# Attention edge pass of a four-layer graph network: LayerNorm sums, variance and power at other places of the step, the edge-row product on VectorE, the segment marks on ScalarE, head scalars on 96 rows

## What is computed

```
s_n, v_n = equivariant_layernorm(s, v)                 # per node: mean and variance of 64 scalars, rms of the vectors
msg = (s_n @ Ws_src)[src] + (s_n @ Ws_dst)[dst]        # the same for the vectors
w1  = rbf @ W_rbf                                      # per edge
m1  = tensor_product(msg, y0, y1, w1)                  # products with the edge's spherical harmonics y
a   = sum(leaky(m1_s @ W_alpha) * alpha_dot)           # 4 heads
ex  = exp(a - segment_max(a, dst)[dst]); den = segment_sum(ex, dst)
val = m1 @ W_val; val_v *= sigmoid(val_s @ Wg); val_s = sigmoid(val_s)
h   = tensor_product(val, y0, y1, w2) @ W_vlin         # head scalars (64) and head vectors (96)
agg = segment_sum(ex / den[dst] * h, dst)              # then a projection, and node + projection(agg)
```

## Time and profile before

| | |
|---|---|
| median of 3 runs | 4730.02 us (4730.01 to 4737.36) |
| the profiled execution | 4743.81 us, span 4742.0 us |
| busy over the span | PE 3709.4 (78%), DVE 3285.3 (69%), ACT 2442.6 (52%), POOL 3346.5 (71%) |
| mean granted TensorE clock | 0.904 |

### The profile page before, as it was taken

The page is one execution under the profiler, slowest core; times in us unless marked ns, Lnnn a source line. Parts: engine busy times, 40 slices in busy tenths (PEclk is TensorE's granted clock), DMA queues, the critical chain, the costliest instruction groups (busy, mean ns, idle before and its releaser), DMA issues. The chain is left out here.

```text
span 4742.0 us, 73825 instructions
## 1 busy us (share of the span) xinstructions
PE 3709.4 (78%) x14102; PEld 1795.8 (38%) x14102; DVE 3285.3 (69%) x8309; ACT 2442.6 (52%) x7488; POOL 3346.5 (71%) x3644
## 2 busy tenths in 40 slices
PE   1999997775999999999910288888798789887665
PEld 0333334553333444444300133333566333333444
DVE  1566666774887898888868545554799455445999
ACT  0233324776555555555457534333699333333777
POOL 1566666997686787788546566666588567666888
PEclk9999998998999999999855589888899898988999
DMA  9222225886454554444379622222798222224886
GB/s 403 67 67 70 67 68 167 275 273 179 115 127 108 127 128 127 127 127 127 88 249 364 229 68 65 67 67 64 240 324 298 70 66 69 66 66 133 251 252 212
DMA packets 585572, 718.24 MB, mean 151 GB/s; under 512 B 79012, under 2 KB 409194, under 8 KB 585224
## 3 DMA queue, kind: packets, MB, share of 16 engines
q1 hardware_dynamic: 492812, 536.17, 37.6%
q0 software_dynamic: 86400, 142.71, 11.0%
q10 hardware_dynamic: 6268, 38.40, 2.0%
HBM read 488.77 MB, written 245.93 MB: 155 GB/s over the span
## 5 line engine op out<-in xcount | busy, mean ns | idle before, releaser
L548 POOL DMA_INDIRECT aggregates<-agg_out,scatter_index x600 | 613.9, 1023 | 402.9 <-issue 247.6
L1296 ACT ACTIVATE y_chunk<-residual,ln_minus_mean_rstd,ln_rstd 128x160 f32<-128x160 f32 x1568 | 701.4, 549 | 201.9 <-POOL ln_minus_mean_rstd L1369 140.9
L1365 POOL TENSOR_TENSOR ln_rstd<-ln_var_eps,minus_half 128x4 f32<-128x4 f32 x392 | 504.7, 1287 | 104.5 <-ACT ln_var_eps L1305 66.7
L531 POOL DMA_INDIRECT gathered<-x_layer,gather_index x400 | 393.3, 983 | 177.7 <-issue 116.5
L1260 PE MATMUL psum<-self_weights,x_chunk_T 128*128 128x160 f32 (+1 forms) x2352 | 414.5, 320 | 57.2 <-ACT x_chunk_T L1319 54.1
L624 PE MATMUL psum<-identity,scaled_x 128*128 128x128 f32 x600 | 146.1, 282 | 378.2 <-ACT scaled_x L570 352.9
L1461 DVE BATCH_NORM_STATS2 ln_stats<-residual 128x6 f32<-128x160 f32 x1568 | 390.5, 311 | 6.8
L1260 PEld LDWEIGHTS psum<-self_weights,x_chunk_T 128*128 128x128 f32 x2352 | 347.7, 192 | 93.3 <-ACT x_chunk_T L1319 53.5
L570 ACT ACTIVATE scaled_x<-gathered,sh_times_attr 128x160 f32<-128x160 f32 x400 | 138.4, 417 | 459.5 <-DVE sh_times_attr L681 305.3
L647 PE MATMUL psum<-hidden,weights 64*128 64x512 f32 x300 | 182.8, 692 | 187.8 <-ACT hidden L582 130.2
L531 POOL DMA_INDIRECT gathered<-in_x,gather_index x200 | 206.3, 1032 | 166.5 <-ACT scaled_x L570 79.2
(11 more groups left out here) (227 smaller groups left out, 10323.8 us busy)
## 6 DMA issues: line engine op xcount, KB each, us to landing
x_layer<-y_chunk SPq DMA_DIRECT2D x294, 320.0 KB, 4.7
x_chunk<-x_layer SPq DMA_DIRECT2D x294, 320.0 KB, 4.6
agg_chunk<-aggregates SPq DMA_DIRECT2D x196, 320.0 KB, 5.6
sh_rows<-in_sh_big SPq DMA_DIRECT2D x50, 768.0 KB
agg_chunk<-aggregates SPq DMA_DIRECT2D x98, 384.0 KB, 5.8
aggregates<-zero_rows ACTq DMA_DIRECT2D x1, 36864.0 KB
x_chunk<-in_x SPq DMA_DIRECT2D x98, 322.0 KB, 3.4
agg_chunk<-aggregates SPq DMA_DIRECT2D x98, 322.0 KB, 3.9
```

The lines of the kernel that those rows point to most:

```text
L531: eng.indirect_dma_start(gathered[:, par, b, 0:width], None, x_table[l][:, :], bass.IndirectOffsetOnAxis(idx_src[:, par, b:b + 1], 0))\
L548: eng.indirect_dma_start(agg_table[:, :], bass.IndirectOffsetOnAxis(idx_last[:, q, b:b + 1], 0), agg_out[:, q, b, :], None, bounds_check=N ...
L1296: op = eng.activation(y_out[:, buf, b, :], res[:, buf, b, :], ACT.Identity, bias=shift[:, buf, b:b + 1], scale=rstd[:, buf, b:b + 1])
L1365: eng.tensor_tensor(rstd[:, buf, :], var_eps[:, q, :], minus_half[:, 0:T], ALU.pow)\
```

## The change

Setup gains a column `low_col` of -1e30, and the waits for the constants go from 7 to 8. In the attention step:

- VectorE: LN sums and square of group s-1 and the product `z_rows` of s-2 come first in the step, ahead of the denominator scan. Variance and epsilon come behind the two scans, ahead of the outputs. The message products are split in 2 and 4, with the scaling of the scalar part between; the denominators' epsilon and the reciprocal follow.
- GpSimd: the product and the segment marks are gone. Order: gathers of tiles 0 and 1, scatters, power, gathers of tiles 2 and 3.
- ScalarE: the segment marks, as an activation with scale 1e30 and bias -1e30, between the tanh values and the tanh of the gates.
- TensorE: HS is computed for 96 rows with 96 columns of weights; rows 64 to 95 are read by nobody.

```diff
@@ attn_gpsimd
-                if live(s, 2, NG):
-                    a = s - 2
-                    eng.wait_ge(S["rows1"] if par else S["rows0"], (a - par) * 16 + 32)
-                    wait(eng, S["w_mm"], 6 * a)
-                    eng.tensor_tensor(z_rows[:, :], z_in[:, par, 0, :], z_in[:, par, 1, :], ALU.mult).then_inc(S["z"], 1)
-                if live(s, 0, NG):
-                    gather((2,))
                 if live(s, 1, NG):
                     ...
                 if live(s, 0, NG):
-                    gather((3,))
-                if live(s, 3, NG):
-                    b_ = s - 3
-                    wait(eng, S["carried"], b_)
-                    eng.tensor_scalar(neg[:, :], goes_on[0:96, b_ * GE:b_ * GE + GE], -1.0, 1e30, ALU.add, ALU.mult)\
-                       .then_inc(S["neg"], 1)
+                    gather((2, 3))
@@ attn_scalar
                     eng.activation(th[64:128, :], pbank("AV")[64:128, :], ACT.Tanh, scale=0.5).then_inc(S["th"], 1)
+                    wait(eng, S["carried"], g)
+                    eng.activation(neg[:, :], goes_on[0:96, bass.ds(g * GE, GE)], ACT.Identity, bias=low_col[0:96, 0:1],
+                                   scale=1e30).then_inc(S["neg"], 1)
                     eng.wait_ge(S["gt_mm"], at(S["gt_mm"], g + 1))
@@ attn_tensor
-                    eng.matmul(pbank("HS", 64), X("Q1")[0:64, 0:64], q_y[0:64, 0, :], start=True, stop=False)
+                    eng.matmul(pbank("HS", 96), X("Q1")[0:64, 0:96], q_y[0:64, 0, :], start=True, stop=False)
                     eng.matmul(pbank("HV", 96), X("Q1")[64:128, 0:96], q_y[64:128, 0, :], start=True, stop=False)
                     eng.matmul(pbank("HV", 96), X("Q2")[:, 0:96], q_y[:, 1, :], start=False, stop=False)
                     eng.wait_ge(S["vy"], at(S["vy"], 4 * d + 4))
-                    eng.matmul(pbank("HS", 64), X("HD")[0:96, 0:64], vy[:, 1, :], start=False, stop=True)\
+                    eng.matmul(pbank("HS", 96), X("HD")[0:96, 0:96], vy[:, 1, :], start=False, stop=True)\
                        .then_inc(S["hs_mm"], 1)
                     eng.matmul(pbank("HV", 96), V("H0")[0:96, 0:96], vy[:, 0, :], start=False, stop=False)
@@ attn_vector: new first blocks of the step
             def step(s, par):
+                if live(s, 1, NG):
+                    g, q = s - 1, 1 - par
+                    wait(eng, S["gather1"] if q else S["gather0"], (g - q) * 64 + 128)
+                    wait(eng, S["square"], g)
+                    for side, rows in enumerate((gathered, gathered_d)):
+                        op = eng.tensor_reduce(ln_sum[:, side, :], rows[:, q, :, 0:64], AX.X, ALU.add)
+                    op.then_inc(S["sums"], 1)
+                if live(s, 1, NG):
+                    g = s - 1
+                    eng.wait_ge(S["sums"], at(S["sums"], g + 1))
+                    wait(eng, S["variance"], g)
+                    eng.tensor_tensor(ln_sq[:, :, :], ln_sum[:, :, :], ln_sum[:, :, :], ALU.mult).then_inc(S["square"], 1)
+                if live(s, 2, NG):
+                    a = s - 2
+                    wait(eng, S["rows1"] if par else S["rows0"], (a - par) * 16 + 32)
+                    wait(eng, S["w_mm"], 6 * a)
+                    eng.tensor_tensor(z_rows[:, :], z_in[:, par, 0, :], z_in[:, par, 1, :], ALU.mult).then_inc(S["z"], 1)
@@ attn_vector: the products, split around the scaling (L1125)
+                def products(first, after):
+                    if live(s, 2, NG):
+                        g = s - 2
+                        eng.wait_ge(S["m_copied"], at(S["m_copied"], 2 * g + 2))
+                        wait(eng, S["vv_mm"], g)
+                        for k, (name, n, m) in list(enumerate((("B1", 128, m_s), ("B2", 128, m_s), ("C", 96, m_v),
+                                                               ("D", 96, m_v), ("F", 96, m_v), ("G", 96, m_v))))[first:after]:
+                            eng.wait_ge(S["w_mm"], at(S["w_mm"], 6 * g + k + 1))
+                            eng.tensor_tensor(pr[0:n, k, :], m[0:n, :], pbank(name, n), ALU.mult).then_inc(S["prods"], 1)
+                products(0, 2)
                 if live(s, 1, NG):
                     ...
+                products(2, 6)
+                if live(s, 4, NG):
+                    g = s - 4
+                    eng.wait_ge(S["den_t"], at(S["den_t"], g * 64 + 64))
+                    wait(eng, S["rec_out"], g * 16)
+                    eng.tensor_scalar(rec[:, :], den_t[:, :], 1e-16, None, ALU.add).then_inc(S["den_e"], 1)
```

More of the change, by code:

```diff
@@ L323, in apart @@
         def apart(eng):
-            eng.wait_ge(P["consts"], 7)
+            eng.wait_ge(P["consts"], 8)
         def apart_from(eng, value):
@@ L1062, in step @@
                        .then_inc(S["scan_v"], 1)
-                if live(s, 5, NG):
-                    g, q = s - 5, 1 - par
-                    eng.wait_ge(S["rden"], at(S["rden"], g * 48 + 48))
-                    eng.wait_ge(S["scan_s"], at(S["scan_s"], g + 1))
-                    eng.wait_ge(S["scan_v"], at(S["scan_v"], g + 1))
-                    wait(eng, S["r_mm"], g)
-                    eng.tensor_tensor(o_s[:, :], sum_s[0:64, q, :], rden[0:64, :], ALU.mult).then_inc(S["o_s"], 1)
-                    eng.tensor_tensor(o_v[:, :], sum_v[:, q, :], rden[:, :], ALU.mult).then_inc(S["o_v"], 1)
-                if live(s, 1, NG):
-                    g, q = s - 1, 1 - par
-                    wait(eng, S["gather1"] if q else S["gather0"], (g - q) * 64 + 128)
-                    wait(eng, S["square"], g)
-                    for side, rows in enumerate((gathered, gathered_d)):
-                        op = eng.tensor_reduce(ln_sum[:, side, :], rows[:, q, :, 0:64], AX.X, ALU.add)
-                    op.then_inc(S["sums"], 1)
-                if live(s, 3, NG):
-                    g = s - 3
-                    eng.wait_ge(S["val"], at(S["val"], g + 1))
-                    eng.scalar_tensor_tensor(out=lk[0:64, :], in0=lk[0:64, :], scalar=0.2, in1=pbank("AV", 64),
-                                             op0=ALU.mult, op1=ALU.max).then_inc(S["leaky"], 1)
-                if live(s, 1, NG):
-                    g = s - 1
-                    eng.wait_ge(S["sums"], at(S["sums"], g + 1))
-                    wait(eng, S["variance"], g)
-                    eng.tensor_tensor(ln_sq[:, :, :], ln_sum[:, :, :], ln_sum[:, :, :], ALU.mult).then_inc(S["square"], 1)
                 if live(s, 1, NG):
@@ L1098, in step @@
                     eng.tensor_scalar(ln_var[:, :, :, :], ln_e2[:, :, :, :], EPS, None, ALU.add).then_inc(S["eps"], 1)
+                if live(s, 5, NG):
+                    g, q = s - 5, 1 - par
+                    eng.wait_ge(S["rden"], at(S["rden"], g * 48 + 48))
+                    eng.wait_ge(S["scan_s"], at(S["scan_s"], g + 1))
+                    eng.wait_ge(S["scan_v"], at(S["scan_v"], g + 1))
+                    wait(eng, S["r_mm"], g)
+                    eng.tensor_tensor(o_s[:, :], sum_s[0:64, q, :], rden[0:64, :], ALU.mult).then_inc(S["o_s"], 1)
+                    eng.tensor_tensor(o_v[:, :], sum_v[:, q, :], rden[:, :], ALU.mult).then_inc(S["o_v"], 1)
+                if live(s, 3, NG):
+                    g = s - 3
+                    eng.wait_ge(S["val"], at(S["val"], g + 1))
+                    eng.scalar_tensor_tensor(out=lk[0:64, :], in0=lk[0:64, :], scalar=0.2, in1=pbank("AV", 64),
+                                             op0=ALU.mult, op1=ALU.max).then_inc(S["leaky"], 1)
                 if live(s, 3, NG):
```

23 lines of the change are left out of this document (6 added, 17 removed).

## The result

| | us |
|---|---|
| kernel before, on the same chip | 4736.31 median of 6 runs (4730.01 to 4745.69) |
| changed kernel | 4756.42 median of 6 runs (4752.31 to 4769.48) |
| ratio | 1.0046, 95% interval 1.0029 to 1.0062 |
| profiled execution, span | 4756.1, that of before 4742.0 |

The change made the kernel slower by 0.46%. I had forecast 4676 us and 4645 to 4714 as the range.

The account below looks back on a forecast made before the run. Bound: a ring from TensorE's value product through LN and GpSimd's power to the transposes. VectorE's and TensorE's new laps plus clock falls took steps from 23.91 to 22.8 us; 49 steps gain 54 us, 4730.0 to 4676, range 4645 to 4714.

Parts of the forecast that it names:

- The gap: TensorE's 1.10 us idle before the transposes each step, waiting on the LN chain; earlier LN work was to remove it.
- the scan: VectorE's scan slowed by GpSimd's edge-row product; moving the product was to take 1.09 us a step off VectorE.
- the head pair: First two head products on TensorE, to run side by side with 96 weight columns: 1.0 us less per step.
- The new laps: Step after the change: VectorE 22.3 us, TensorE 20.9 us of work in a ring of 22.1 us.
- The clock: Falls of TensorE's granted clock, taken in one step of three after the change: 22.8 us a step on average.
- rival A: Clock falls vanish (79 us gained, 4651) or come every second step (4688); inside the forecast, together 0.73.
- The power beside two-input instructions: GpSimd's power running beside VectorE's `out_scalars` and `out_vectors`; the forecast expected no blocking, both taking 1.33 us as ever.
- Rival D: GpSimd's power blocks VectorE for 2.9 us: 64 us slower, 4794; with all else slower, chance 0.07.
- B: Clock falls in every step: 23.8 us a step, 5 us gained, 4725; chance 0.10.
- C: The first two head products on TensorE still queue: 20 us gained, 4710; chance 0.10.
- The step that failed: Reordered GpSimd gathers costed at nothing, and SyncE's earlier release for its next loads given no price.
- My own condition for being wrong: A full-clock step above 22.8 us, from an unseen ring, most likely variance waiting for the last squares.

Follow-up runs that it names:

- g1: Kernel before with only the head scalars' products on 96 columns of weights: 4688.04 us, ratio 0.9922.
- j2: Kernel before with only SyncE's five y-row loads moved one step later, behind the denominators' loads: 4727.86 us, ratio 0.9987.
- g2: Kernel before with only the edge rows' product moved from GpSimd to the head of VectorE's step: 4722.76 us, ratio 0.9988.
- j1: Changed kernel with SyncE's five y-row loads moved one step later, behind the denominators' loads: 4663.35 us, ratio 0.9845 against the kernel before.
- h4: Changed kernel with the segment marks back on GpSimd and the constant column not declared: 4726.9 us, ratio 0.9978 against the kernel before.
- i4: Changed kernel with product and marks back on GpSimd and no constant column, leaving head pair and LN part: 4758.91 us, ratio 0.9980 against the kernel before.
- i3: Kernel before with the constant column declared but no instruction that sets it: 4775.42 us, ratio 1.0032.
- g3: Kernel before with only the segment marks moved from GpSimd to ScalarE, with their constant column: 4746.73 us, ratio 1.0038.
- g4: Changed kernel with the edge rows' product back on GpSimd, between scatters and power: 4695.6 us, ratio 0.9928 against the kernel before.
- i1: Changed kernel with the edge rows' product later on VectorE, behind the epsilon instruction: 4792.39 us, ratio 1.0068 against the kernel before.
- h1: Changed kernel with the constant column widened to 64 bytes per partition: 4756.05 us, ratio 1.0042 against the kernel before.

## Why the prediction was wrong

*The gap, the scan and the head pair: right.* The gap went; the scan is 1.25 us in each step; the pair starts together. From the first to the fiftieth transposes g1 takes 1126.4 us where the kernel before takes 1171.5, 0.92 us a step; I took 1.0 for the pair. But g1 has lost the held signals too. Against j2, which has lost them alone (1157.1), the pair gives 0.63 us a step, with the clock's falls still in both. g2 takes 1154.0 us, 0.36 a step less than before, where I took 0.5 off VectorE; against j2 it is 0.06, so that the product alone gave next to nothing beyond the held signals that went.

*The new laps: right, where nothing is held.* j1 has 22.4 us a step, with 20.8 us of work on TensorE; I had 22.3 and 20.9. Its 49 steps are 88.7 us shorter than before, more than the 79 of the forecast's best end; 14.4 of them j2 gains without any part of the change. TensorE's idle time lies in three short pieces, ahead of L966, L970 and L989 (0.77, 0.27, 0.48 us), as put down for "what the profile will show".

*The clock: mis-sized, on the safe side.* I took one fall in three steps. In j1 the clock stands at 1.00 throughout, which was the end of rival A, 4651 us. The changed kernel had 0.98 with 3 to 4 us of idle time in each step, so its clock cost next to nothing either.

*The power beside two-input instructions: right.* In j1 the power starts at 1808.86 and `out_scalars` at 1808.87, and the two VectorE instructions take 0.74 and 0.67 us. Rival D did not come, and neither did B or C. That the change would be slower stood at 0.07, and it came by another way than D's.

*The step that failed.* Of GpSimd's queue I wrote that "the last rows are requested at about the same time as now. [...] I cost this at nothing", and of SyncE that it "is released earlier", with no price. Both shifts move transfers against each other, and I summed only the work of the compute engines and the waits between them. That TensorE's signals could come late, and that the place of SyncE's loads beside GpSimd's transfers could decide it, was in no term and in no rival. It costs 24.36 - 22.37 = 2.0 us a step here, or by the two stretches 1172.9 - 1082.8 = 90 us. My own condition for being wrong (a full-clock step above 22.8) was met, but for another ring than the one I named: in the changed kernel variance never waits for the last squares.

*It was to be seen.* The kernel before had held signals in single steps. Its waits from 1320 to 2290 us:

```profile
ACT message_scalars L920 <- remote: 12.8, 3, 4.6
...
DVE vector_message L1054 <- remote: 8.0, 4, 2.8
```

and in the step that begins at 1439.56 (L979, whose result VectorE's L1054 reads, was over at 1447.87, and L984 at 1448.72):

```profile
1452.27 0.68 DVE L1054 TENSOR_TENSOR vector_message<-exp_a,psum 96x512 f32<-96x512 f32 x1 [2.84 <-remote]
...
1445.61 6.57 SPq L818 DMA_DIRECT2D sh_row_pairs<-in_sh_big  x4
```

ScalarE's L920, which reads L984's result, waits 4.63 us for "remote" until 1453.09. From the start of SyncE's first `sh_row_pairs` load to that of the fourth it is over 3 us in 29 of 40 steps of the kernel before, and 2.1 in j1. These waits stood in a list that I had before me, and I passed over them and over SyncE's issue times. They were a sign and no measure: only 4 of those 29 steps have a signal over 1.5 us late, while the changed kernel has one in each step, with even loads.

*The 15 us outside.* I cost the constant column at nothing. All 14 kernels that declare it have a node update of 296.7 to 301.3 us, all 6 that don't (the kernel before, g1, g2, h4, i4, j2) one of 281.0 to 282.7. i3 shows that the instruction that sets it has no part in it. That is the whole difference between the two profiled executions (14.1 us, where the node update is 15.1 longer); without it the held signals and the gains would have cancelled to within a few us. j1 pays it too; j1 without the column wasn't run.

*What stays open.* Why TensorE's signals are held, and how the place of SyncE's loads decides it, is not settled. Nor is which part of the change brings it: each of the head pair, the product and the marks alone has nothing held (g1 to g3), the pair with the LN part has 299 us (i4), and with the marks on ScalarE besides, 0 (g4, on another chip). GpSimd's row alone is not enough (g4 and j1 have rows of twelve and nothing held), nor is SyncE's place beside it (g1 to g3 have it, and nothing held). Taking the y loads out of the stretch freed both kernels in which it was tried. Both runs also put the y loads ahead of the store and the loads of the reciprocal denominators, and that order may have a part in it. The numbers also depend on the chip: the kernel before took 4729 us in the median on one and 4760 on another, where i1 to i4 ran, so that i4's held signals may not come on each. Nor is it shown why tiles 32 or 64 bytes further on cost 5.5% of the transfer rate.

The Trainium skill (DMA: Bandwidth & Descriptors, section How a descriptor splits into AXI transactions) says that a transaction begins at a multiple of 256 bytes, so that a descriptor which doesn't start at one fetches bytes that it doesn't use. The page speaks of reads, and no run here tests it. By it, and by the tiles' sizes, `agg_chunk` is the tile that would tell: each of its rows of 640 bytes starts 128 bytes past such a multiple before and touches three blocks of 256 bytes, and 160 or 192 past one with the column, where it touches four; for `x_chunk` and `y_chunk` the count hardly changes. This is an estimate, and it fits that 32 and 64 bytes cost the same. A column of 128 or 256 bytes, by which the count is three again, would test it and wasn't run.

## What to carry to other kernels

Before costing a move at nothing, look at what the DMA-issuing queues do in the same microseconds: a wait on TensorE whose releaser is "remote" on a single core can mean that a signal came late, and a shift can make it the rule. For loads with a step or two to spare, try a stretch in which no other queue is issuing; here it gave 2%. Price one part against a kernel that has the same held signals, not just against the one before. And a tile of a few bytes is not free where it moves the tiles of a DMA-bound stage: declare it last (not tried here), or compare the GB/s of that stage with and without it.

## What was not expected of the hardware

- TensorE's semaphores rose up to 7 us (1824.21 to 1831.24) behind the recorded ends of the matmuls, several then 0.06 us apart, while VectorE's came within 0.03 us in the same stretch.
- Four SyncE loads that go out in 2.6 us took 6.6 to 6.8 us beside GpSimd's indirect transfers in single steps of the kernel before and of i3, but not in the changed kernel.
- Moving SBUF tiles by 32 or 64 bytes took a DMA-bound stage from 365 to 345 GB/s (h1, with 64 bytes, has 345 too):

```profile
2473.00:2673.00 200.00, 0.00 (x0) 0.00 (x0) 154.74 (x630) 142.19 (x420) 116.29 (x139) 0.50 1.12 344
...
2423.00:2623.00 200.00, 0.00 (x0) 0.00 (x0) 163.44 (x667) 150.42 (x444) 126.43 (x148) 0.50 1.10 365
```

The first of these two rows is i3 (column declared), the second j2 (none), each some 40 us into its node update.
